# Scores in PSUM banks by row half of the array, and one group's probabilities scaled by ScalarE

## The chip, the cores and the metric

The kernel runs on one core of a Trainium2 chip. The metric is the device time of one execution in microseconds: 998.45 us is the median of three runs of the kernel before (997.99 to 999.91). The engines are named as in the profile: PE is TensorE's matmul side and PEld its weight loads, DVE is VectorE, ACT is ScalarE, POOL is GpSimd and SP is SyncE, which only issues transfers here.

## The reference, cut to what matters

Four layers are added to `x` (64 elements of a batch, 64 tokens each, 512 wide) one after the other. The change lies in the third, attention over a window of 256 earlier keys and the tokens' own 64:

```
q, k, v = x @ Wq.T, x @ Wk.T, x @ Wv.T          # 8 heads of q, 4 groups of k and v, 64 wide
q, k = rope(rms(q)), rope(rms(k))
k_blocks, v_blocks = paged cache with the new k and v written in
scores = einsum('bghtd,bgsd->bghts', q, k_all) * SCALE
scores = where(kpos <= pos and kpos > pos - 256, scores, -inf)
p = softmax(scores)
o = einsum('bghts,bgsd->bghtd', p, v_all)
x = x + o @ Wo.T
x = x + einsum('bct,bcd->bdt', x, weights[subjects]) + bias[subjects]
```

## The kernel before

**Two phases.** Phase one, the first 524 us, works on pairs of elements: expert matmul, adapter, the projections to q, k and v, and the write of the new keys and values to DRAM. Phase two, the rest, takes one element `b` at a time through `phase_two(b, j, s)`, written once for each engine. Every engine runs its own list in the order of the text; only semaphores tie the lists together. An element's stages are spread over several steps: step `b` of TensorE computes the scores of `b`, transposes the probabilities of `b - 1`, and multiplies them with the values of `b - 1`. Below, "even" and "odd" are the parity of `b`, and an element's time is that of its scores.

**TensorE's step.** `scores` (L755), the first half of the next element's keys transposed (`transpose_keys`, L732 and L733), in even steps six matmuls of the output projection (`project`, L803), the ten transposes of the probabilities (L771 for the two blocks of the tokens' own keys into `ps_pt2`, L778 for the eight others into `ps_pt`), the second half of the keys, then in odd steps six matmuls of the projection and in even steps the last layer's matmul (L839), and last `values` (L791, L796), whose last matmul raises `pv_done`.

**The scores.** Each of the four groups `g` has a score of 128 rows (two heads, 64 tokens) by `NK` = 320 keys. Queries and keys of groups 0 and 2 lie in partitions 0 to 63, those of 1 and 3 in 64 to 127, so matmuls of the two kinds use different row halves of the array and run at the same time. A PSUM bank holds 512 columns. `S0` says where a group's 320 columns begin; a group that crosses a bank's edge is computed in two pieces. Before, group 0 lies in bank 0, group 2 in banks 0 and 1, group 3 in banks 1 and 2, group 1 in bank 2: bank 1 gets columns from both halves of the array. So the piece of group 2 in bank 1 raises `s_shared`, and before the last piece, that of group 3 in bank 1, TensorE waits for `s_shared`, which it has raised itself.

**VectorE's step.** `masked(g)` (L1243) adds the mask to a group's scores and finds the extreme; it waits for all four `s_done` of the element and raises `sm_ready`. Between these lie the last layer's sum (L1255, odd steps), `copy_first` (L1225), which takes the first of the transposed probabilities out of PSUM, and the residual sum (L1268, even steps). Then come `recip` (L1276), four products that scale each group's probabilities (L1280, `prob_ready`), `make_mask` for the next element, and last `split_outputs` (L1232, `ot_lo`), which waits for ScalarE's `ot_hi`. The next step's `masked(0)` stands right behind `split_outputs`.

**ScalarE's step.** The first half of the keys copied (L921), the exponentials (L931), `copy_own` and `copy_second` (L943, L938), the second half of the keys, and last `ot_hi` (L968), the rounded output of `b - 1`, which waits for `pv_done`.

**GpSimd** issues the indirect transfers that gather keys and values (L501 from the cache, L537 and L548 from the new rows). They are paced by `pt_done`, `kt_done`, `prob_ready` and `s_done`.

## Time and profile before

| | |
|---|---|
| median of three runs | 998.45 us |
| the profiled execution's own time | 999.21 us |
| its span, first to last instruction | 997.4 us |
| phase two, from the first scores | 524.2 us to the end |
| PE busy | 941.9 us, 94% of the span |
| DVE, ACT, POOL busy | 602.1, 386.0, 512.9 us |
| mean granted TensorE clock | 0.991 of full speed |

The profile is of one execution. A line such as L755 is a line of the kernel file; a group of instructions is named by line, engine, operation and the tiles it writes and reads. Busy time is not the bound by itself: what counts is what an engine waited for before it started, which the views of waits and the timeline tell. Ends of matmuls are modelled in this profile, so a matmul's start is firmer than its end. A wait is put down to the event that the profile saw last; "remote" means that it saw none that fits.

### The profile page before, as it was taken

The page shows a single profiled execution, that of the slowest core. Times are in us where ns is not written, and L with a number is a line of the kernel's source. Part 1 is how long each engine was busy: PE and PEld are TensorE (multiplying, and loading weights), DVE is VectorE, ACT ScalarE, POOL GpSimd, SP SyncE. Part 2 cuts the span into 40 slices and gives each one's busy share as a digit, 9 for nine tenths or more (in the row PEclk, how much of TensorE's full clock was granted, in tenths as well). Part 3 has the DMA queues.
Part 4 walks back from the last instruction along what each step waited for, and adds up shares of the span by engine and source line. Part 5 has one row for each costly group of instructions (what it writes and reads, how often), then busy time and mean ns, then how long its engine had stood idle before and what let it go on. Part 6 is the DMA issues. An engine that isn't in the chain of part 4 may idle for free.

```text
span 997.4 us, 22018 instructions
## 1 busy us (share of the span) xinstructions
PE 941.9 (94%) x6253; PEld 683.0 (68%) x6253; DVE 602.1 (60%) x1788; ACT 386.0 (39%) x1061; POOL 512.9 (51%) x469
## 2 busy tenths in 40 slices
PE   5899999999999999999977999999899999999997
PEld 4566766766766766766755777777677777777775
DVE  5434434656656644356455667776676777677775
ACT  2122122221221221221225556565565656565653
POOL 1245555455455477564565455555455555555530
PEclk9999999999999999999999999999999999999999
DMA  9879877767777667778355565566466565566641
GB/s 299 271 260 315 294 277 265 261 217 271 247 229 274 235 235 260 239 245 281 133 171 172 155 194 165 182 188 184 142 186 190 161 211 192 167 181 191 201 137 44
DMA packets 96458, 212.48 MB, mean 213 GB/s; under 512 B 29051, under 2 KB 35160, under 8 KB 88226
## 3 DMA queue, kind: packets, MB, share of 16 engines
q1 hardware_dynamic: 66434, 145.53, 43.7%
q0 software_dynamic: 25088, 57.74, 19.8%
q10 hardware_dynamic: 4896, 8.73, 2.4%
q8 instruction: 17, 0.28, 0.1%
q14 instruction: 23, 0.19, 0.1%
HBM read 204.39 MB, written 33.86 MB: 239 GB/s over the span
## 4 chain that ended last, share of the span: by engine, by line
PE 91%; DVE 2%; issue 2%; DMA 2%; ACT 1%; another core or an unknown queue 1%; SPq 1%; POOL 0%; ACTq 0%; DVEq 0%; POOLq 0%
PE banks L589 11%; PE banks L755 10%; PE banks L803 10%; PE banks L707 9%; PE banks L791 6%; PE banks L628 6%; PE banks L636 6%; PE banks L638 6%; PE banks L778 5%; PE banks L732 3%; PE banks L839 3%; PE banks L697 3%; PE banks L712 3%; PE banks L796 2%; PE banks L599 2%
## 5 line engine op out<-in xcount | busy, mean ns | idle before, releaser
L548 POOL DMA_INDIRECT ring<-new_rows,idx x128 | 130.8, 1022 | 85.0 <-DVE big L1280 33.9
L460 POOL TENSOR_TENSOR rms<-ss,neg_half 128x12 f32<-128x12 f32 x31 | 70.8, 2284 | 182.0 <-DVE ss L1185 181.0
L931 ACT ACTIVATE big<-big,neg_max 128x320 f32<-128x320 f32 x256 | 141.6, 555 | 5.1 <-DVE neg_max L1243 3.8
L1243 DVE CUSTOM_DVE_ANT_0 big<-banks,mask 128x320 f32<-128x320 f32 x256 | 114.6, 486 | 17.7 <-PE banks L755 13.1
L755 PE MATMUL banks<-kt,q_in 64*128 64x192 f32 (+2 forms) x768 | 103.7, 366 | 20.9 <-remote 12.3
L589 PE MATMUL banks<-ring 128*64 128x512 f32 x512 | 117.1, 599 | 3.0 <-DMA ring<-in_w 3.0
L872 ACT ACTIVATE x2t_hi<-banks 128x512 fp32r<-128x512 f32 x32 | 19.1, 597 | 235.7 <-PE banks L599 235.7
L755 PEld LDWEIGHTS banks<-kt,q_in 64*128 64x128 f32 x768 | 79.0, 188 | 44.5 <-remote 16.9
L501 POOL DMA_INDIRECT ring<-in_kvrows,idx x64 | 61.1, 955 | 63.3 <-PE banks L755 45.8
L537 POOL DMA_INDIRECT ring<-new_rows,idx x64 | 61.4, 960 | 57.7 <-PE banks L778 36.2
L589 PEld LDWEIGHTS banks<-ring 128*64 128x64 f32 x512 | 33.9, 136 | 81.4 <-issue 80.3
L921 ACT ACTIVATE kt<-banks 128x384 f32<-128x384 f32 x128 | 61.8, 483 | 69.6 <-PE banks L733 55.3
L1280 DVE TENSOR_SCALAR big<-big,recip 128x320 f32<-128x320 f32 x256 | 84.2, 392 | 2.3
L791 PEld LDWEIGHTS banks<-pt,ring 128*64 128x64 f32 x1024 | 54.9, 136 | 39.3 <-DVE pt L1225 22.0
L1138 DVE TENSOR_TENSOR x<-banks,x_in 128x512 f32<-128x512 f32 x32 | 22.1, 691 | 95.4 <-PE banks L589 93.8
L791 PE MATMUL banks<-pt,ring 128*64 128x128 f32 x1024 | 70.0, 279 | 4.0 <-ACT pt L938 1.9
L968 ACT ACTIVATE ot_hi<-banks 128x256 fp32r<-128x256 f32 x64 | 24.5, 383 | 120.9 <-remote 67.7
L1232 DVE TENSOR_TENSOR ot_lo<-banks,ot_hi 128x256 fp32r<-128x256 f32 x64 | 27.0, 421 | 73.3 <-ACT ot_hi L968 59.0
L904 ACT ACTIVATE sq<-banks 128x512 f32<-128x512 f32 x31 | 18.5, 597 | 130.6 <-PE banks L638 130.6
L778 PE MATMUL banks<-ident,big 128*128 128x128 f32 x512 | 67.9, 277 | 0.2 <-DVE ot_lo L1232 0.2
L636 PE MATMUL banks<-wqkv_hi,x2t_lo 128*128 128x512 f32 x248 | 66.4, 390 | 0.0
L638 PE MATMUL banks<-wqkv_lo,x2t_hi 128*128 128x512 f32 x248 | 66.3, 389 | 0.0
(169 smaller groups left out, 2015.3 us busy)
## 6 DMA issues: line engine op xcount, KB each, us to landing
ring<-in_w SPq DMA_DIRECT2D x62, 1024.0 KB, 6.4
ring<-in_xt SPq DMA_DIRECT2D x32, 256.0 KB
x_in<-in_x SPq DMA_DIRECT2D x32, 256.0 KB, 5.5
bias_in<-in_b SPq DMA_DIRECT2D x64, 128.0 KB, 5.5
x_dram<-x SPq DMA_DIRECT2D x32, 256.0 KB, 5.1
q_dram<-q_t ACTq DMA_DIRECT2D x32, 256.0 KB
new_rows<-kv_out SPq DMA_DIRECT2D x32, 256.0 KB, 5.0
q_in<-q_dram SPq DMA_DIRECT2D x32, 256.0 KB
```

The lines of the kernel that those rows point to most:

```text
L548: pool.indirect_dma_start(out=kv[:, s, c, :], out_offset=None, in_=new_rows, in_offset=bass.IndirectOffsetOnAxis(ap=idx[:, b, 1 + c:2 + c] ...
L589: last = nc.tensor.matmul(ps_l0[T * h:T * h + T, :], xt[:, s, c, T * h:T * h + T], w0[:, 2 * s + h, c * D:(c + 1) * D], start=(c == 0), st ...
L636: nc.tensor.matmul(ps_out[:, :], x2t_lo[:, c, :], wqkv_hi[:, c, n0:n0 + D], start=False, stop=False)
L638: last = nc.tensor.matmul(ps_out[:, :], x2t_hi[:, c, :], wqkv_lo[:, c, n0:n0 + D], start=False, stop=(c == DC - 1))
L707: nc.tensor.matmul(ps_l1[:, :], x_part[:, c, :], w_part[:, c, :], start=(c == 0 and x_part is x1t_hi and w_part is w1_hi), stop=False)
L755: return nc.tensor.matmul(banks[:, S0[g] + n0:S0[g] + n1], q_in[r0:r0 + HD, s % 4, g // 2, :], kt[r0:r0 + HD, s % 2, g // 2, k0 + n0:k0 + ...
L778: last = nc.tensor.transpose(ps_pt[p][:, (q * 2 + c) * P:(q * 2 + c + 1) * P], prob[:, r % 2, (5 * p + 3 * q + c) * P:(5 * p + 3 * q + c + ...
L791: nc.tensor.matmul(ps_o[p][HD * q:HD * q + HD, :], kv[:, r, c, v0:v0 + HD], pt[:, p, PLACE[2 * p + q] % 2, c, :], start=(c == 0), stop=Fal ...
L803: last = nc.tensor.matmul(out[:, n0:n1], o_part[:, pair_s, c, :], w_part[:, c, n0:n1], start=(c == 0 and n == 0), stop=(c == DC - 1 and n ...
L931: nc.scalar.activation(prob[:, s % 2, PLACE[g] * NK:(PLACE[g] + 1) * NK], sm[:, s % 2, g, :], ACT.Exp, bias=neg_max[:, s % 2, g:g + 1], sc ...
L1243: V.tensor_tensor_reduce(sm[:, s % 2, g, :], ps_s[g], mask[:, s % 2, k0:k0 + NK], 1.0, 3.0e38, ALU.add, ALU.min, accum_out=neg_max[:, s % ...
L1280: V.tensor_scalar(own_row, own_row, recip[:, s % 2, g:g + 1], None, ALU.mult).then_inc(prob_ready, 1)
```

## The change

Four things change together.

- `S0` and the order of the pieces: groups 1 and 3 (the upper row half) now lie in banks 0 and 1, groups 2 and 0 (the lower half) in banks 2 and 3. No bank gets columns from both halves. `s_shared` and TensorE's wait for it are gone. There are six pieces as before, of the same sizes, now in pairs of equal size, one of each half.
- Bank 3 now holds the last 128 columns of group 0, so the transposed keys (`ps_kt`) move from bank 3 to bank 6, and the transposes of the own keys' probabilities (`ps_pt2`) from bank 6 into the rest of bank 3. Those two transposes now stand between the first four and the last four of the others, and wait for `sm_ready` of the same step's `masked(0)`, which reads bank 3.
- The waits of ScalarE's `copy_own` and VectorE's `copy_first` follow the new order of the transposes.
- Group 0's probabilities are scaled by ScalarE, in place, between the second copy of the keys and `ot_hi`; VectorE scales the other three. `prob0_ready` tells TensorE and VectorE of it.

```
-S0 = (0, 3 * BANK - NK, NK, 3 * BANK - 2 * NK)
+S0 = (2 * BANK + NK, 0, 2 * BANK, NK)
...
-        ps_kt, ps_pt, ps_pt2, ps_x = ps[3], ps[4:6], ps[6][:, 0:GP * P], ps[7]
+        ps_kt, ps_pt, ps_pt2, ps_x = ps[6], ps[4:6], ps[3][:, P:P + GP * P], ps[7]
...
-                        pool.wait_ge(prob_ready, G * n + 2)
+                        pool.wait_ge(prob_ready, (G - 1) * n + 2)
...
-                    piece(2, BANK - NK, NK).then_inc(s_shared, 1)
-                    piece(1, 0, NK).then_inc(s_done, 1)
-                    piece(0, 0, NK).then_inc(s_done, 1)
-                    piece(3, P, NK)
-                    piece(2, 0, BANK - NK).then_inc(s_done, 1)
-                    pe.wait_ge(s_shared, b + 1)
-                    piece(3, 0, P).then_inc(s_done, 1)
+                    for g in (2, 1):
+                        piece(g, 0, NK).then_inc(s_done, 1)
+                    for g in (0, 3):
+                        piece(g, 0, BANK - NK)
+                    for g in (0, 3):
+                        piece(g, BANK - NK, NK).then_inc(s_done, 1)
...
-                    pe.wait_ge(prob_ready, G * b)
-                    wait(pe, pt2_ready, b - 1)
-                    for p in range(GP):
-                        last = nc.tensor.transpose(ps_pt2[:, p * P:(p + 1) * P], prob[:, r % 2, (5 * p + 2) * P:(5 * p + 3) * P], ident[:, :])
-                    last.then_inc(pt_done, 1)
+                    pe.wait_ge(prob_ready, (G - 1) * b)
+                    pe.wait_ge(prob0_ready, b)
...
+                        if p == 0:
+                            wait(pe, pt2_ready, b - 1)
+                            if on(b, 0, NB):
+                                pe.wait_ge(sm_ready, G * b + 1)
+                            for n in range(GP):
+                                last = nc.tensor.transpose(ps_pt2[:, n * P:(n + 1) * P], prob[:, r % 2, (5 * n + 2) * P:(5 * n + 3) * P],
+                                                           ident[:, :])
+                            last.then_inc(pt_done, 1)
...
-                    act.wait_ge(pt_done, 3 * b - 2)
+                    act.wait_ge(pt_done, 3 * b - 1)
...
+                if on(b, 0, NB):
+
+                    act.wait_ge(recip_ready, b + 1)
+                    first_row = prob[:, s % 2, PLACE[0] * NK:(PLACE[0] + 1) * NK]
+                    nc.scalar.activation(first_row, first_row, ACT.Copy, scale=recip[:, s % 2, 0:1]).then_inc(prob0_ready, 1)
...
-                    dve.wait_ge(pt_done, 3 * b - 1)
+                    dve.wait_ge(pt_done, 3 * b - 2)
...
-                    wait(dve, prob_ready, G * b - G)
+                    wait(dve, prob_ready, (G - 1) * b - (G - 1))
+                    wait(dve, prob0_ready, b - 1)
...
-                    for g in range(G):
+                    for g in range(1, G):
```

On TensorE, in an odd step of the loop, these rows stand before, from the scores to the second keys (`big` holds the probabilities, `ring` the gathered keys):

```order
L755 MATMUL banks<-kt,q_in 128x128 [waits kt_ready]
L755 MATMUL banks<-kt,q_in 128x320 x2
L755 MATMUL banks<-kt,q_in 128x192 x2
L763 REGISTER_ALU
L755 MATMUL banks<-kt,q_in 128x128 [waits s_shared]
L252 REGISTER_ALU [waits g_new4,g_old4]
L732 MATMUL banks<-ident,ring 128x128 [waits kt_ready]
L732 MATMUL banks<-ident,ring 128x128
L733 MATMUL banks<-ident,ring 128x2x64
L771 MATMUL banks<-ident,big 128x128 [waits pt2_ready,prob_ready]
L771 MATMUL banks<-ident,big 128x128
L778 MATMUL banks<-ident,big 128x128 [waits pt0_ready,ot_ready]
```

And the same place now, where L774 is what L778 was, and L782 what L771 was:

```order
L755 MATMUL banks<-kt,q_in 128x192 x2
L755 MATMUL banks<-kt,q_in 128x128 x2
L252 ISA [waits g_new4,g_old4]
L732 MATMUL banks<-ident,ring 128x128 [waits kt_ready]
L732 MATMUL banks<-ident,ring 128x128
L733 MATMUL banks<-ident,ring 128x2x64
L767 REGISTER_ALU
L774 MATMUL banks<-ident,big 128x128 [waits ot_ready,pt0_ready,prob0_ready,prob_ready]
L774 MATMUL banks<-ident,big 128x128 x3
L780 REGISTER_ALU [waits pt2_ready]
L782 MATMUL banks<-ident,big 128x128 [waits sm_ready]
L782 MATMUL banks<-ident,big 128x128
```

The wait for `s_shared` in front of the last piece is gone. A wait for `sm_ready` has come seven transposes behind the scores (three of keys, four of probabilities); six transposes of probabilities stand behind it.

On ScalarE, at the end of an odd step, these rows stand before:

```order
L921 ACTIVATE kt<-banks 128x384 [waits s_done,kt_done]
L252 REGISTER_ALU [waits pv_done]
L968 ACTIVATE ot_hi<-banks 128x4x64 [waits wo_done]
L919 ISA
L252 ISA [waits kt_done]
```

and these now:

```order
L925 ACTIVATE kt<-banks 128x384 [waits s_done,kt_done]
L970 ACTIVATE big<-big,recip 128x320 [waits recip_ready]
L252 REGISTER_ALU [waits pv_done]
L977 ACTIVATE ot_hi<-banks 128x4x64 [waits wo_done]
L923 ISA
L252 ISA [waits kt_done]
```

The scaling of group 0 (L970) has come in front of `ot_hi`, behind the copy of the keys.

## Rows read from the trace of the kernel before

**Rows 1.** The page: the chain that ended last, by engine.

```profile
PE 91%; DVE 2%; issue 2%; DMA 2%; ACT 1%; another core or an unknown queue 1%; SPq 1%; POOL 0%; ACTq 0%; DVEq 0%; POOLq 0%
```

**Rows 2.** Waits of TensorE: engine, line and who was waited for; us in all, times, longest.

```profile
PE banks L755 <- remote: 12.3, 13, 2.4
...
PE banks L755 <- PE banks L755: 6.1, 14, 0.6
```

**Rows 3.** Timeline: start us, us, engine, line, operation [idle before <-releaser]; one odd element.

```profile
574.71 0.45 PE L796 MATMUL banks<-pt,ring 64*64 64x128 f32 x8
...
575.09 1.35 PE L755 MATMUL banks<-kt,q_in 64*128 64x128 f32 x10
...
575.45 1.01 POOL L548 DMA_INDIRECT ring<-new_rows,idx  x1 [0.30 <-issue]
...
576.42 0.38 ACT L968 ACTIVATE ot_hi<-banks 128x256 fp32r<-128x256 f32 x1 [2.46 <-PE banks L796]
...
576.83 0.42 DVE L1232 TENSOR_TENSOR ot_lo<-banks,ot_hi 128x256 fp32r<-128x256 f32 x1 [1.95 <-issue]
...
577.16 0.49 PE L755 MATMUL banks<-kt,q_in 64*128 64x128 f32 x2 [0.72 <-remote]
...
577.77 0.49 DVE L1243 CUSTOM_DVE_ANT_0 big<-banks,mask 128x320 f32<-128x320 f32 x1 [0.51 <-PE banks L755]
...
579.05 0.38 PE L732 MATMUL banks<-ident,ring 128*128 128x128 f32 x2
```

**Rows 4.** Timeline: the next odd element.

```profile
591.33 0.48 PE L755 MATMUL banks<-kt,q_in 64*128 64x128 f32 x2 [0.56 <-PE banks L755]
...
591.34 0.38 ACT L968 ACTIVATE ot_hi<-banks 128x256 fp32r<-128x256 f32 x1 [3.32 <-remote]
...
591.76 0.42 DVE L1232 TENSOR_TENSOR ot_lo<-banks,ot_hi 128x256 fp32r<-128x256 f32 x1 [2.49 <-ACT ot_hi L968]
...
592.18 0.49 DVE L1243 CUSTOM_DVE_ANT_0 big<-banks,mask 128x320 f32<-128x320 f32 x1
...
593.22 0.38 PE L732 MATMUL banks<-ident,ring 128*128 128x128 f32 x2
```

**Rows 5.** Timeline: the even element between the two.

```profile
582.28 1.35 PE L755 MATMUL banks<-kt,q_in 64*128 64x128 f32 x12
...
582.62 0.38 ACT L968 ACTIVATE ot_hi<-banks 128x256 fp32r<-128x256 f32 x1 [0.59 <-PE banks L796]
...
583.94 0.49 DVE L1243 CUSTOM_DVE_ANT_0 big<-banks,mask 128x320 f32<-128x320 f32 x1
...
585.35 0.38 PE L771 MATMUL banks<-ident,big 128*128 128x128 f32 x2
...
586.44 0.38 PE L732 MATMUL banks<-ident,ring 128*128 128x128 f32 x2
...
586.88 0.96 POOL L537 DMA_INDIRECT ring<-new_rows,idx  x1 [1.23 <-PE banks L778]
```

**Rows 6.** Timeline of one long stop, and its 7 us by engine, clock and DMA.

```profile
713.78 0.48 PE L755 MATMUL banks<-kt,q_in 64*128 64x128 f32 x2 [2.36 <-remote]
...
714.64 0.49 DVE L1243 CUSTOM_DVE_ANT_0 big<-banks,mask 128x320 f32<-128x320 f32 x1
...
718.50 0.59 PE L732 MATMUL banks<-ident,ring 128*128 128x128 f32 x2
...
714.00:721.00 7.00, 7.00 (x42) 5.48 (x41) 5.32 (x18) 4.11 (x13) 2.67 (x3) 0.76 0.36 85
```

**Rows 7.** The page: groups by line, busy us, mean ns of one, idle before.

```profile
L1280 DVE TENSOR_SCALAR big<-big,recip 128x320 f32<-128x320 f32 x256 | 84.2, 392 | 2.3
...
L931 ACT ACTIVATE big<-big,neg_max 128x320 f32<-128x320 f32 x256 | 141.6, 555 | 5.1 <-DVE neg_max L1243 3.8
```

**Rows 8.** Timeline: the last element's probabilities, scaled and transposed.

```profile
982.25 1.27 DVE L1280 TENSOR_SCALAR big<-big,recip 128x320 f32<-128x320 f32 x4
...
983.58 0.44 PE L771 MATMUL banks<-ident,big 128*128 128x128 f32 x2 [1.04 <-DVE big L1280]
```

More of the change, by code:

```diff
@@ L214, in build @@
         g_new = [sem(f"g_new{i}") for i in range(KV_SLOTS)]
-        s_shared, s_done, kt_done, pt_done, pv_done = sem("s_shared"), sem("s_done"), sem("kt_done"), sem("pt_done"), sem("pv_done")
+        s_done, kt_done, pt_done, pv_done = sem("s_done"), sem("kt_done"), sem("pt_done"), sem("pv_done")
         wo_done, l3_done = sem("wo_done"), sem("l3_done")
@@ L220, in build @@
         x3_ready, x4_ready = sem("x3_ready"), sem("x4_ready")
-        e_ready, kt_ready, prob_ready = sem("e_ready"), sem("kt_ready"), sem("prob_ready")
+        e_ready, kt_ready, prob_ready, prob0_ready = sem("e_ready"), sem("kt_ready"), sem("prob_ready"), sem("prob0_ready")
         st_out = [sem(f"st_out{i}") for i in range(2)]
```

## The prediction

> **What bounds the kernel now.** I read the chain that ended last first: 91% of it is TensorE [rows 1], so what counts is TensorE's work and the few places where it stands. The waits of TensorE come next. Its largest waits in the whole kernel are both at L755, the scores: 12.3 us in 13 places put to "remote" and 6.1 us in 14 put to L755 itself, 18.4 us in 27 places [rows 2]. That is the most that the removed wait can be seen to cost. Last I read the timeline of phase two, element by element, and there the parity matters.
>
> In an even element all twelve score instructions (each piece is two) run through in 1.35 us with no stop; `masked(0)` starts 1.66 us behind the scores' start and the probabilities' transposes only 3.07 us behind it, since six projection matmuls lie between [rows 5]. In an odd element ten of the twelve run, TensorE stands for 0.72 us, and the last piece starts at 577.16, 2.07 us behind the start [rows 3]. The signal that it waits for belongs to the first piece, which was through some 1.5 us before. Not only that signal is late. `values` ended at 575.16 (574.71 + 0.45) and `ot_hi`, which needs only its signal and an idle ScalarE, starts at 576.42. In the next odd element `ot_hi` starts at 591.34, after 3.32 us of idle time, and TensorE's last piece at 591.33, at the same moment [rows 4]. So in odd elements TensorE's signals reach everybody late, all at once, and they do so just behind a run of GpSimd's gathers (L548 to 576.46 [rows 3]). That is a time which the change doesn't touch: this run of gathers begins with L537 at 586.88, released by the transposes of the even element before [rows 5].
>
> **The self wait.** It goes with its 0.72 or 0.56 us of standing. What is late next is the new wait: TensorE runs on through three transposes of keys and four of probabilities and then needs `masked(0)` of the same element. In an odd element `masked(0)` hangs on the same late signals twice: through all four `s_done`, and through `pv_done`, `ot_hi` and `ot_lo`, since `ot_lo` stands right in front of it on VectorE. So I compare one point of the step, the start of the second keys (second L732), behind which both kernels do the same.
>
> Second kind of odd element, `pv_done` as late as the rest [rows 4]: `ot_lo` 591.76 + 0.42 = 592.18 = start of `masked(0)`, both before and now. It takes 0.49. From VectorE's end to TensorE's next start there are 0.06 us (L1280 ends at 982.25 + 1.27, L771 starts at 983.58 [rows 8]). Then six transposes at 0.11 each (ten take 586.44 - 585.35 = 1.09 [rows 5]) and 0.06 for the first after a stop (0.44 for two in [rows 8] against 0.38 in [rows 5]): 592.18 + 0.49 + 0.06 + 0.66 + 0.06 = 593.45. Before it was 593.22. The change loses 0.23 here. In about half of these elements `ot_hi` follows its signal faster by up to 0.08, and the loss is 0.16; mean 0.20.
>
> First kind, `pv_done` early enough [rows 3]: `ot_lo` ended at 577.25, and `masked(0)` waited till 577.77 for the last piece, which was behind the self wait. Now it waits for the late signals alone, about 577.35: 577.35 + 0.49 + 0.06 + 0.72 = 578.62 against 579.05. The change gains 0.4 here.
>
> Counted along the timeline from 575 to 970 us, the first kind comes 4 times (scores at 575.09, 631.6, 688.5 and 949.0) and the second 23 times. Sum: 23 x 0.20 - 4 x 0.4 = 4.7 - 1.6 = +3.1 us. The odd elements at 543.8 and 561.4, of the start of phase two, add about 0.2 each: +0.4.
>
> **The long stops.** At two even elements (scores at 550.7 and 710.1) the signals are later still; at the second TensorE stands 2.36 us, and in the 7 us behind it the granted clock is 0.76 on average, below its 2.4 GHz level for part of the time [rows 6]. There the projection lies in front of the new wait, so TensorE works while it would have stood: second keys at 714.64 + 0.49 + 0.06 + 0.72 = 715.91, against 718.50, of which part is the low clock. Worth 1.2 us without the clock and 2.6 with it, each; but which parity a long stop hits is chance. I take half of 2 x 1.2: -1.2. In odd elements such a stop brings the 0.2 as above.
>
> **Even elements.** The new wait is over before it is reached: `masked(0)` ends at 583.94 + 0.49 = 584.43, the transposes that need it come after 585.35 [rows 5]. 0.
>
> **The scaling.** VectorE saves one of four products, 84.2 / 256 = 0.33 us each [rows 7]. VectorE waits in odd elements before `ot_lo` (1.95 and 2.49 us idle [rows 3, 4]), so the saving is lost there; in even ones it starts `masked(0)` a little earlier, which nobody on the path waits for. ScalarE gets 64 products of 128 x 320. No row shows this operation on ScalarE; the nearest are L931, the same tile with an exponential and a sum (0.555 us [rows 7]), and L968, half as many columns from PSUM (0.38 [rows 3]). I take 0.5. It lies in front of `ot_hi`, where ScalarE idles 0.59 us at the tightest place shown [rows 5] and 2.46 or 3.32 in odd ones [rows 3, 4]. Cost 0; at 0.555 with its start it just fits 0.59. If that cover is short by 0.1 us in even elements, `ot_lo` still isn't the last thing that `masked(0)` needs to be early for, as above. At the very end TensorE waits for the scaling [rows 8]: three products end 0.33 earlier while ScalarE does the fourth beside them: -0.2, taken once. The bounds of the whole edit are -0.4 and, if every odd `ot_hi` came 0.1 later, +2.7.
>
> The Trainium skill, page "VectorE: DVE Perf Modes", section "The TRN2 errata — SBUF-src ops pay a fixed extra latency per instruction", speaks against this move: it gives ScalarE 224 cycles plus a cycle per element at 1.2 GHz for SBUF to SBUF, VectorE 58 plus the elements at 0.96 GHz. For 320 elements that is 0.45 us on ScalarE against 0.39 on VectorE, an estimate from that page. By it the product would cost more engine time where it goes than where it leaves, and the sum would be the same, since 0.45 fits the idle time too.
>
> **The pieces.** Same six sizes, both halves get 640 columns as before, and the halves already ran side by side (1.35 us for all [rows 5]). 0; bounds -0.1 and +0.1 an element, -6 and +6 in all, of which I expect nothing since an even element shows no gap. The moved tiles cost nothing by themselves. The first two `s_done` come a little earlier, but L501 waits for late signals in odd elements and for GpSimd itself in even ones: 0.
>
> **The sum.** 3.1 + 0.4 - 1.2 - 0.2 = +2.1 us on 999.21, the profiled execution's own time; its span of 997.4 grows by as much. The median of the runs shown is 998.45, 0.76 lower, so I predict 998.45 + 2.1 = 1000.6 us. For a single measurement of this kernel 0.2%, 2.0 us, is what can be told from no change, and the forecast lies at that edge.
>
> **Rivals.** *The late signals go with the wait* (faster). Then an odd element is like an even one: `masked(0)` 1.66 us behind the scores, seen 0.55 later at 2.21; TensorE is there at 1.35 + 7 x 0.11 = 2.12 and waits 0.1. 18.4 - 27 x 0.1 = 15.7 gained: 983 us. For it: late signals and a standing TensorE come in the same elements. Against it: in even elements, with no stop, `ot_hi` also starts only 0.34 us behind the scores' start (582.62 against 582.28 [rows 5]), though its source is done before them, and in odd ones the lateness ends just behind the gathers. A milder form, in which all odd elements become of the first kind, gives 27 x 0.4 = 11: 988 us.
>
> *The clock* (slower). TensorE's idle time in an odd element moves behind the seven transposes and grows by 0.2 us, to 1.0 to 1.4. A stop of 2.36 us was followed by half-level clock for part of the next 7 us [rows 6], 0.24 x 7 = 1.7 us of full speed lost. If stops of 1.4 us did the same, even in a third of the odd elements, that is 9 x 1.7 = 15: 1016 us. Against it: the mean granted clock is 0.991 over the whole span, with 27 stops of 0.7 us on average in it. [...]
>
> *The array itself is late*, not the signals, so the change doesn't free what it says. The gain of the first kind goes: +1.2 more, 1002 us. Against it: the late signals arrive together while the pieces' starts are spread over 1.3 us. The Trainium skill, page "Perfetto Trace Analysis", section "Tensor Engine Instruction (MATMUL, LD_WEIGHTS)", says that a matmul's end in a profile is an estimate and its signal is pushed when PSUM has acknowledged the writes. By that rule the array may be the late one, and the sum would be this rival's; the trace here doesn't decide it.
>
> **Chances.** Forecast 0.66 (own range 998 to 1003: slower in 0.32, same in 0.30, faster in 0.04). Late signals gone, in either form, 0.20, all faster. Clock 0.07, all slower. Array late 0.07, slower 0.05 and same 0.02. So faster 0.24, same 0.32, slower 0.44. The range runs from 988, the milder form, to 1005.
>
> **What would show it.** Right: in odd elements ten rows become twelve with no gap, TensorE then stands at L782 for about 1.2 us put to VectorE's L1252, and the second keys start 3.7 to 4.3 us behind the scores. `ot_hi` in odd elements still starts 1.3 us or more behind the scores' start. Wrong: no wait at L782 above 0.2 us, or an odd `ot_hi` 0.3 us behind; or a granted clock clearly below 0.99; or gaps before `ot_hi` in which ScalarE is busy with L970.

## The result, and the profile after

The change makes the kernel slower by 0.44%: the ratio of after to before is 1.0044, 95% interval 1.003 to 1.0059, so 4.4 us (3.0 to 5.9). The medians of 20 runs each are 1003.81 us after and 998.56 before; two of after's runs were disturbed, at 3032.14 and 1522.51 us, and count in no comparison (the median of the other 18 is 1003.10). In a later set of runs the same two kernels gave 1.0043 (1.0023 to 1.0062). I had said 1000.6 us, +2.1: the direction and the range hold, the size is half of what was measured. The span of the profiled execution is 1002.8 us, 5.4 more than before, with a mean granted clock of 0.997 (before 0.991); over the 18 runs of after that count it lies between 0.990 and 0.997.

The chain that ended last, by engine, first. Before it was TensorE for 91% [rows 1].

```profile
PE 71%; issue 9%; ACT 8%; another core or an unknown queue 6%; DVE 4%; DMA 2%; SPq 1%; ACTq 1%; DVEq 0%
```

A fifth of the span has gone from TensorE to others and to "issue". Something that TensorE waits for is now on the path. Its waits (line, who was waited for, us in all, times, longest):

```profile
PE banks L774 <- DVE ot_lo L1241: 28.8, 31, 1.4
...
PE banks L843 <- DVE bias_in L1277: 5.3, 16, 0.6
...
PE banks L755 <- issue: 4.0, 4, 1.7
...
PE banks L782 <- DVE neg_max L1252: 0.4, 2, 0.2
```

The 18.4 us at L755 [rows 2] have become 4.0. In their place stand 28.8 us in 31 places at L774, the first four transposes of the probabilities, and they are put to `ot_lo`. The wait that I had named, L782 for `masked(0)`, has 0.4 us, in no place more than 0.2. The prediction names just that as a sign of being wrong ("no wait at L782 above 0.2 us"), and it has come. The timeline of the odd element that answers to [rows 4] (start us, us, engine, line, operation, idle before and releaser):

```profile
589.50 1.01 POOL L548 DMA_INDIRECT ring<-new_rows,idx  x1 [0.30 <-issue]
...
589.64 1.35 PE L755 MATMUL banks<-kt,q_in 64*128 64x320 f32 x12
...
590.93 0.44 PE L732 MATMUL banks<-ident,ring 128*128 128x128 f32 x2
...
591.38 0.38 ACT L977 ACTIVATE ot_hi<-banks 128x256 fp32r<-128x256 f32 x1 [2.46 <-remote]
...
591.80 0.42 DVE L1241 TENSOR_TENSOR ot_lo<-banks,ot_hi 128x256 fp32r<-128x256 f32 x1 [2.51 <-ACT ot_hi L977]
...
592.22 0.49 DVE L1252 CUSTOM_DVE_ANT_0 big<-banks,mask 128x320 f32<-128x320 f32 x1
...
592.48 0.63 PE L774 MATMUL banks<-ident,big 128*128 128x128 f32 x4 [1.00 <-DVE ot_lo L1241]
...
592.94 0.38 PE L782 MATMUL banks<-ident,big 128*128 128x128 f32 x2
...
593.16 0.60 PE L774 MATMUL banks<-ident,big 128*128 128x128 f32 x4
...
593.60 0.38 PE L732 MATMUL banks<-ident,ring 128*128 128x128 f32 x2
```

The twelve score rows run through with no gap. The signals are as late as they were: `ot_hi` (L977) starts 1.74 us behind the scores. TensorE is through with the first keys at about 591.3 and then stands for `ot_ready`, which `ot_lo` raises (591.80 + 0.42), until 592.48. L782 follows 0.46 us behind the first of the four transposes, with hardly a wait. From `ot_hi` to the second keys it takes 593.60 - 591.38 = 2.22 us; before it was 593.22 - 591.34 = 1.88 [rows 4]. I call an element late when its `ot_hi` starts more than 1.1 us behind its scores; behind 570 us these are 27 after and 28 before, all odd but the one of the long stop. Their median is 2.21 after and 1.95 before: +0.26 us.

The median hides that before had the prediction's two kinds. In the 22 elements of the second kind of [rows 4] that are late in both kernels the way was 1.91 us on average (1.87 or 1.96 each) and is 2.22 now, +0.31 each. In the four of the first kind of [rows 3] it was 2.64 and is 2.21, -0.43 each. After has only one kind left. Summed over the elements it is +6.9 and -1.7, together +5.2 us.

The even element, for [rows 5]:

```profile
581.80 0.55 ACT L970 ACTIVATE big<-big,recip 128x320 f32<-128x320 f32 x1
...
582.32 1.36 PE L755 MATMUL banks<-kt,q_in 64*128 64x320 f32 x12
...
582.58 0.38 ACT L977 ACTIVATE ot_hi<-banks 128x256 fp32r<-128x256 f32 x1 [0.23 <-PE banks L800]
...
585.40 0.60 PE L774 MATMUL banks<-ident,big 128*128 128x128 f32 x4
...
586.49 0.38 PE L732 MATMUL banks<-ident,ring 128*128 128x128 f32 x2
```

Up to the second keys it is as before within 0.05 us (586.49, before 586.44). ScalarE's scaling (L970) ends 0.23 us ahead of `ot_hi`, which starts 0.26 us behind the scores (before 0.34).

Element by element, the scores of the two kernels start together at 575.1 us. At the element of the long stop they are 2.7 us apart (710.1 and 712.8), behind it 0.3 (728.0 and 728.4), and at the last element 5.3 (976.66 and 981.97). That is 0.28 us in each pair of elements, 9.5 pairs and 17.5 pairs, with 2.4 us won at the one long stop between: 7.6 us lost elsewhere.

Where those 7.6 us lie depends on where one measures from. From scores to scores, the 28 odd elements grew by 1.1 us in all and the 27 even ones (without that of the long stop) by 6.1, of which some 5.4 lie between an even element's second keys and the next scores. There the residual sum (L1277) starts 4.09 us behind the scores in the median, before 3.82, and TensorE waits for it. But beside that stretch run the gathers that lead to the next late signal: L537 begins behind the even element's transposes, and the odd `ot_hi` comes 4.25 us behind it on average. So I cut the same time at the signals, in 26 pairs of elements without the one of the long stop:

| after minus before, us in 26 pairs | first trace of after | second trace of after |
|---|---|---|
| odd second keys to even transposes | -0.9 | -0.9 |
| to the start of L537 | -0.9 | -1.2 |
| to the odd `ot_hi` | +3.6 | +0.1 |
| `ot_hi` to the odd second keys | +5.7 | +5.9 |
| together | +7.5 | +3.9 |

Only the way from `ot_hi` to the second keys grows by the same amount in both traces. The time from L537 to `ot_hi` differs by as much between the two executions of after as between one of them and before. That the even elements' wait for the residual sum costs nothing of its own, because it runs beside the gathers, is my reading of this table. It isn't shown: no run takes that wait away alone, and where the time from L537 to the odd scores is longer, that from L537 to `ot_hi` tends to be longer too.

The groups that answer to [rows 7], the long stop of [rows 6] and the end of [rows 8]:

```profile
L1290 DVE TENSOR_SCALAR big<-big,recip 128x320 f32<-128x320 f32 x192 | 63.1, 385 | 2.4
...
L970 ACT ACTIVATE big<-big,recip 128x320 f32<-128x320 f32 x64 | 36.0, 562 | 2.2 <-DVE recip L1286 0.7 <-issue 0.5
```

```profile
712.76 1.36 PE L755 MATMUL banks<-kt,q_in 64*128 64x320 f32 x12
...
716.19 0.39 ACT L977 ACTIVATE ot_hi<-banks 128x256 fp32r<-128x256 f32 x1 [3.24 <-remote]
...
717.28 0.63 PE L774 MATMUL banks<-ident,big 128*128 128x128 f32 x4 [0.37 <-DVE ot_lo L1241]
...
718.40 0.38 PE L732 MATMUL banks<-ident,ring 128*128 128x128 f32 x2
```

```profile
989.16 0.63 PE L774 MATMUL banks<-ident,big 128*128 128x128 f32 x4 [1.32 <-DVE ot_lo L1241]
```

### The profile page after: what moved, and what is told of

The parts are those of the page before. It is cut to its first block, busy times and chain, and to the rows that moved or that the text cites. A ratio compares the mean times of both kernels' runs of the same rounds, so it can differ in the third digit from the quotient of the medians.

```text
span 1002.8 us, 22139 instructions
## 1 busy us (share of the span) xinstructions
PE 930.4 (93%) x6253; PEld 665.0 (66%) x6253; DVE 583.9 (58%) x1724; ACT 419.5 (42%) x1125; POOL 515.0 (51%) x469
## 4 chain that ended last, share of the span: by engine, by line
PE 71%; issue 9%; ACT 8%; another core or an unknown queue 6%; DVE 4%; DMA 2%; SPq 1%; ACTq 1%; DVEq 0%
PE banks L589 11%; PE banks L707 8%; PE banks L807 6%; PE banks L628 6%; PE banks L636 6%; PE banks L638 6%; PE banks L795 4%; PE banks L774 4%; PE banks L800 3%; ACT big L935 3%; PE banks L697 3%; PE banks L712 3%; PE banks L755 3%; PE banks L599 2%
## 5 line engine op out<-in xcount | busy, mean ns | idle before, releaser
L548 POOL DMA_INDIRECT ring<-new_rows,idx x128 | 131.3, 1026 | 83.0 <-PE banks L755 37.9
L774 PE MATMUL banks<-ident,big 128*128 128x128 f32 x512 | 77.8, 274 | 28.8 <-DVE ot_lo L1241 28.8
L537 POOL DMA_INDIRECT ring<-new_rows,idx x64 | 61.6, 962 | 65.4 <-PE banks L774 56.9
L755 PE MATMUL banks<-kt,q_in 64*128 64x320 f32 (+2 forms) x768 | 88.7, 362 | 4.0 <-issue 4.0
L774 PEld LDWEIGHTS banks<-ident,big 128*128 128x128 f32 x512 | 59.5, 141 | 39.6 <-issue 33.2
L755 PEld LDWEIGHTS banks<-kt,q_in 64*128 64x128 f32 x768 | 66.4, 188 | 25.1 <-issue 15.8
L450 POOL TENSOR_TENSOR x_in<-x_in,bias_in 128x512 f32<-128x512 f32 x32 | 41.0, 1280 | 54.8 <-DMA ring<-in_rope 48.1
```

The source lines that it names most:

```text
L548: pool.indirect_dma_start(out=kv[:, s, c, :], out_offset=None, in_=new_rows, in_offset=bass.IndirectOffsetOnAxis(ap=idx[:, b, 1 + c:2 + c] ...
L755: return nc.tensor.matmul(banks[:, S0[g] + n0:S0[g] + n1], q_in[r0:r0 + HD, s % 4, g // 2, :], kt[r0:r0 + HD, s % 2, g // 2, k0 + n0:k0 + ...
L774: last = nc.tensor.transpose(ps_pt[p][:, (q * 2 + c) * P:(q * 2 + c + 1) * P], prob[:, r % 2, (5 * p + 3 * q + c) * P:(5 * p + 3 * q + c + ...
```

## The experiments

All carry a short edit of one of the two kernels. Beside each ratio I give what the trace says of one point, the way from the start of `ot_hi` to the second keys in the late elements (median of 27 to 29): 1.95 us before, 2.21 after. The ratios' intervals are some 0.5% wide, so most of them don't tell one edit from another; this way does.

**The scaling taken back.** The kernel after, with VectorE scaling all four groups.

```
-                    first_row = prob[:, s % 2, PLACE[0] * NK:(PLACE[0] + 1) * NK]
-                    nc.scalar.activation(first_row, first_row, ACT.Copy, scale=recip[:, s % 2, 0:1]).then_inc(prob0_ready, 1)
...
-                    pe.wait_ge(prob_ready, (G - 1) * b)
-                    pe.wait_ge(prob0_ready, b)
+                    pe.wait_ge(prob_ready, G * b)
...
-                    for g in range(1, G):
+                    for g in range(G):
```

> The kernel after, with VectorE scaling all four groups' probabilities as before; banks, order of the transposes and the missing wait stay as after. Theory A (the loss is where the own-key transposes stand relative to TensorE's wait for ot_ready: they were done in front of it and now lie behind it, 0.22 us and a restart in each of the 27 or so odd elements with late signals): about as after, 3.5 to 5.5 us slower than before, L774 still stands about 1 us on L1241 in odd elements. Theory B (ScalarE's scaling, 0.55 us in front of ot_hi, makes ot_hi late): at most 1 us slower than before. A little may be lost on either by a VectorE step 0.3 us longer.

Ratio to before 1.0032 (1.0009 to 1.0054): most of the loss stays without the scaling, as theory A says, though 3.2 us is a little under its 3.5 to 5.5, and the interval holds after's 1.0044 too. A late element, `ot_lo` and the first transposes:

```profile
604.58 0.42 DVE L1235 TENSOR_TENSOR ot_lo<-banks,ot_hi 128x256 fp32r<-128x256 f32 x1 [2.23 <-ACT ot_hi L971]
...
605.10 0.63 PE L773 MATMUL banks<-ident,big 128*128 128x128 f32 x4 [0.71 <-issue]
```

They start 0.52 us behind the start of `ot_lo` (median 0.53), not 0.68: with one wait less in front of them, 0.15 less. The second keys come 2.11 us behind `ot_hi`. So the scaling has a price after all, but through the wait that it needs and not through its 0.56 us.

**The scaling alone.** The kernel before, with the lines above put in.

> The kernel before, with only the scaling of group 0 given to ScalarE. Theory A (order of the transposes): within 1 us of before. Theory B (ScalarE's scaling): 4 to 5 us slower. In the profile the odd ot_hi (L968) starts as before, 1.3 us or more behind the scores' start, under A; later by up to 0.55 us under B.

Ratio 1.0006 (0.9981 to 1.0031), 1.95 us from `ot_hi` to the second keys: no change. `ot_hi` itself starts 1.97 us behind the scores (before 1.79), but the signal that TensorE's last piece waits for is as late, and from the end of the last gather to `ot_hi` it is 0.74 us (before 0.77), so this is the gathers' timing and not the scaling. The extra wait for `prob0_ready` costs nothing here either, since TensorE is busy when it comes to it. Theory B falls.

**The order alone.** The kernel before, with the transposes in the order of after.

```
                     pe.wait_ge(prob_ready, G * b)
-                    wait(pe, pt2_ready, b - 1)
-                    for p in range(GP):
-                        last = nc.tensor.transpose(ps_pt2[:, p * P:(p + 1) * P], prob[:, r % 2, (5 * p + 2) * P:(5 * p + 3) * P], ident[:, :])
-                    last.then_inc(pt_done, 1)
                     wait(pe, ot_ready, b - 1)
                     for p, copied in ((0, pt0_ready), (1, pt1_ready)):
...
                         last.then_inc(pt_done, 1)
+                        if p == 0:
+                            wait(pe, pt2_ready, b - 1)
+                            for n in range(GP):
+                                last = nc.tensor.transpose(ps_pt2[:, n * P:(n + 1) * P], prob[:, r % 2, (5 * n + 2) * P:(5 * n + 3) * P],
+                                                           ident[:, :])
+                            last.then_inc(pt_done, 1)
```

> The kernel before, with only the order of the transposes changed: the first four of the others, then the two own-key ones, then the last four. Banks and TensorE's wait for itself stay. Theory A: slower by 3 to 6 us, the first transposes stand on ot_lo about 1 us in odd elements and the second keys move 0.2 us back. Theory C (banks, and the new wait for sm_ready, cost the time): no change, within 1 us.

Ratio 1.0023 (0.9998 to 1.0049): slower at the edge of what the runs tell, less than theory A's 3 to 6 us, and 2.06 us from `ot_hi` to the second keys. One late element:

```profile
604.21 0.38 ACT L970 ACTIVATE ot_hi<-banks 128x256 fp32r<-128x256 f32 x1 [3.11 <-remote]
...
604.27 0.48 PE L755 MATMUL banks<-kt,q_in 64*128 64x128 f32 x2 [0.34 <-PE banks L755]
...
604.63 0.42 DVE L1234 TENSOR_TENSOR ot_lo<-banks,ot_hi 128x256 fp32r<-128x256 f32 x1 [2.25 <-ACT ot_hi L970]
...
604.69 0.44 PE L732 MATMUL banks<-ident,ring 128*128 128x128 f32 x2
...
605.15 0.63 PE L774 MATMUL banks<-ident,big 128*128 128x128 f32 x4
```

This shows how the two orders differ. Before, everything behind the late signal is TensorE's own work: last piece, first keys, ten transposes, 1.87 to 1.96 us without a stop. Here the transposes that overwrite `ps_o` come 0.2 us earlier in the list than `ot_ready` allows, and wait about 0.1 us, not the expected 1 us, since the last piece and the keys still stand in front. The expected second keys 0.2 us later were 0.11.

**Fewer waits.** The kernel after without the waits for `pt0_ready`, `pt1_ready` and `pt2_ready` of the element before, which `values` has passed already.

```
-                    for p, copied in ((0, pt0_ready), (1, pt1_ready)):
-                        wait(pe, copied, b - 1)
+                    for p in range(GP):
...
-                            wait(pe, pt2_ready, b - 1)
```

> The kernel after, with the waits for pt0_ready, pt1_ready and pt2_ready of the step before left out in front of the transposes (values of the step before has waited for the same counts), so that ot_ready is the last wait of its row. Theory A with a restart made longer by waits in a chain: the gap from the start of ot_lo to the first transposes falls from 0.68 us by about 0.1, in 27 odd elements, 2 to 3 us faster than after. Rival (the chain of waits costs nothing, only the signal's way counts): as after, within 0.7 us.

Ratio to before 1.0022 (0.9994 to 1.0049), where after has 1.0044 and 1.0043 in its two sets of runs. The interval alone decides nothing; the trace has 0.57 us from `ot_lo` to the transposes and 2.11 from `ot_hi` to the second keys, 0.10 less than after, as expected.

**One wait.** The kernel after with `ot_ready` as the only wait in that row.

```
-                    pe.wait_ge(prob_ready, (G - 1) * b)
-                    pe.wait_ge(prob0_ready, b)
+                    if isinstance(b, int) and b < 2:
+                        pe.wait_ge(prob_ready, (G - 1) * b)
+                        pe.wait_ge(prob0_ready, b)
                     wait(pe, ot_ready, b - 1)
```

> The kernel after, with ot_ready as the only wait in front of the first transposes of the probabilities (four before: prob_ready, prob0_ready, ot_ready, pt0_ready; VectorE raises ot_ready of the element before behind everything that the others stand for), and no waits for pt1_ready and pt2_ready behind them. Theory W (each wait in that row costs TensorE about 0.1 us although it is long fulfilled; the traces so far have 0.45 us with two waits, 0.53 to 0.57 with three, 0.68 with four from the start of ot_lo to the transposes behind it): 0.35 us with one, the second keys 1.9 us behind ot_hi in place of 2.21, 27 times 0.3 = 8 us faster than after, so some 3 us faster than the kernel before. Rival (the number of waits is a coincidence, it is where the own-key transposes stand): 0.6 us or more, not more than 2 us faster than after.

Ratio to before 1.0013 (0.9986 to 1.0039), beside 1.0043 for after on the same chip: some 3 us are won back, not 8, with intervals that overlap.

```profile
602.49 0.42 DVE L1240 TENSOR_TENSOR ot_lo<-banks,ot_hi 128x256 fp32r<-128x256 f32 x1 [2.35 <-ACT ot_hi L976]
...
602.92 0.49 DVE L1251 CUSTOM_DVE_ANT_0 big<-banks,mask 128x320 f32<-128x320 f32 x1
...
602.97 0.66 PE L774 MATMUL banks<-ident,big 128*128 128x128 f32 x4 [0.50 <-DVE ot_lo L1240]
...
603.47 0.44 PE L781 MATMUL banks<-ident,big 128*128 128x128 f32 x2
...
604.19 0.38 PE L732 MATMUL banks<-ident,ring 128*128 128x128 f32 x2
```

The first transposes start 0.48 us behind `ot_lo`, not 0.35. Then L781 comes 0.50 us behind them, where it was 0.46 in after: now it is TensorE's wait for `masked(0)` that holds (602.92 + 0.49, and 0.06 to TensorE's start, is 603.47). With the restart behind it this costs 0.1 us, from the first transposes to the second keys 1.21 us in place of 1.12. So the second keys stay 2.11 us behind `ot_hi`. The wait that I had predicted is there; it lies 0.1 us behind the one that bound.

**One wait, in the kernel before.**

```
                     pe.wait_ge(prob_ready, G * b)
-                    wait(pe, pt2_ready, b - 1)
...
-                    for p, copied in ((0, pt0_ready), (1, pt1_ready)):
-                        wait(pe, copied, b - 1)
+                    for p in range(GP):
```

> The kernel before, with prob_ready as the only wait in front of the own-key transposes and ot_ready as the only one in front of the others (pt0_ready, pt1_ready and pt2_ready left out). Theory W: from ot_lo to the transposes 0.35 us in place of 0.45, second keys 1.85 us behind ot_hi in place of 1.95, 27 times 0.1 = 3 us faster than before. Rival: no difference, within 1 us.

Ratio 0.999 (0.9969 to 1.001), and 0.45 and 1.95 us as before: theory W misses here. In the kernel before TensorE is busy from the late signal on, so there was no wait to shorten. What W said of the number of waits holds only where TensorE stands: 0.48 us with one, 0.53 and 0.57 with three, 0.68 with four.

**After once more**, unchanged.

> The kernel after, unchanged, so that g1 can be compared with it on one chip: 3 to 6 us slower than before on either theory, 0.68 us from ot_lo to the first transposes.

1.0043 (1.0023 to 1.0062), 0.68 us and 2.21 us as in its first trace.

**No bursts of gathers.** The kernel before, without L548, and `g_new` counted accordingly.

```
-                    pool.indirect_dma_start(out=kv[:, s, c, :], out_offset=None, in_=new_rows,
-                                            in_offset=bass.IndirectOffsetOnAxis(ap=idx[:, b, 1 + c:2 + c], axis=0),
-                                            bounds_check=NB * T - 1, oob_is_err=False).then_inc(g_new[s], 16)
...
-                    pe.wait_ge(g_new[s], 48 * (j + 1))
+                    pe.wait_ge(g_new[s], 16 * (j + 1))
```

> The kernel before without the two gathers of new rows in columns 0 and 1 of each element (L548): it leaves the batch's new keys and values out of the windows of earlier keys. All waits of GpSimd stay. Theory G (the bursts of gathers hold TensorE's signals back): no odd ot_hi later than 0.5 us behind the scores' start, odd period about 6 us, whole run 20 to 35 us shorter. Rival S (TensorE's wait for itself holds them): odd ot_hi still 1.3 us behind the scores, no shorter than 3 us.

948.76 us, 47 less than before, more than I expected. An odd element:

```profile
592.98 1.36 PE L752 MATMUL banks<-kt,q_in 64*128 64x128 f32 x12
...
593.12 0.38 ACT L965 ACTIVATE ot_hi<-banks 128x256 fp32r<-128x256 f32 x1 [1.26 <-PE banks L793]
...
594.65 0.38 PE L768 MATMUL banks<-ident,big 128*128 128x128 f32 x2
...
595.74 0.38 PE L729 MATMUL banks<-ident,ring 128*128 128x128 f32 x2
```

`ot_hi` starts 0.14 us behind the scores, the last piece has no gap, and TensorE doesn't stand. An odd period is 5.99 us in the median (7.02 before), an even one 6.87 (7.13). Behind 570 us all of TensorE's late signals but one, in an even element, have gone with the gathers, and the kernel still waits for itself. So the lateness comes with the gathers; rival S falls. Part of the 47 us can be the traffic saved, which this run doesn't separate.

**After without them.** The same edit to the kernel after.

> The kernel after without the two gathers of new rows in columns 0 and 1 of each element (L548): it leaves the batch's new keys and values out of the windows of earlier keys, as the kernel before without them did (948.8 us). If the change costs only where TensorE's signals are late: no odd element stands on ot_lo, 1 us slower to 3 us faster than that. If it costs by itself: 951 us or more.

953.28 us, 4.5 more than the kernel before without them. The change costs by itself too, which I had not expected. An odd element:

```profile
591.48 1.36 PE L752 MATMUL banks<-kt,q_in 64*128 64x320 f32 x12
...
592.03 0.42 DVE L1238 TENSOR_TENSOR ot_lo<-banks,ot_hi 128x256 fp32r<-128x256 f32 x1 [1.10 <-ACT ot_hi L974]
...
593.14 0.49 DVE L1249 CUSTOM_DVE_ANT_0 big<-banks,mask 128x320 f32<-128x320 f32 x1 [0.69 <-PE banks L752]
...
593.14 0.60 PE L771 MATMUL banks<-ident,big 128*128 128x128 f32 x4
...
593.70 0.44 PE L779 MATMUL banks<-ident,big 128*128 128x128 f32 x2
...
594.41 0.27 PE L729 MATMUL banks<-ident,ring 128*128 128x128 f32 x1
```

Here `ot_lo` is long done. `masked(0)` starts as TensorE's first transposes do, at 593.14, and L779 needs its result: 593.70, 0.56 us behind, where four transposes take 0.44. With 0.05 for the restart the second keys come 2.93 us behind the scores, not 2.76. That is 0.17 us in nearly every odd element. From the scores at 573.25 us to those at 915.21 without the change, and from 571.59 to 917.50 with it, the difference is 4.0 us: 26 odd elements by 0.17, less 0.6 won in the one even element where the kernel before had a late signal. The two times, of two runs each and on two chips, are 4.5 apart; as ratios to the kernel before on their own chips they are 0.9524 (0.9478 to 0.9571) and 0.9567 (0.9527 to 0.9607), so the times alone don't show the cost, and the traces do. This is the predicted wait, at the predicted place, in a kernel whose signals are on time.

**A later third gather.** The kernel before, with L548's second gather moved behind the next element's scores.

```
-                        pool.wait_ge(prob_ready, G * n + 2)
+                        pool.wait_ge(s_done, G * (n + 1) + 2)
```

> The kernel before, with the third gather of an element's new rows (L548, c = 1) issued by GpSimd only when the second score piece of the next element is done, so that three gathers no longer run back to back into an odd element's scores. Theory G (TensorE's signals come 0.6 to 1.0 us behind the end of back-to-back gathers): odd ot_hi starts 0.2 to 0.4 us behind the scores as in even elements, the odd period falls from 7.0 us by 0.7 to 1.2, the whole by 15 to 30 us. Rival S (the signals are late because TensorE waits for itself): odd ot_hi as late as before, within 2 us of before. Third case: the gathers behind it now delay another signal, gain below 10 us.

Ratio 1.001 (0.9988 to 1.0032). The odd period falls to 6.13 us as theory G has it, though `ot_hi` still starts 0.98 us behind the odd scores and not 0.2 to 0.4, and the even one rises from 7.13 to 8.23: the third case. The burst has only moved to the even elements. One of them, with its scores at 593.39:

```profile
591.66 0.96 POOL L537 DMA_INDIRECT ring<-new_rows,idx  x1 [0.30 <-issue]
...
593.44 1.00 POOL L548 DMA_INDIRECT ring<-new_rows,idx  x1 [0.82 <-remote]
...
594.23 0.52 PE L755 MATMUL banks<-kt,q_in 64*128 64x320 f32 x1 [0.30 <-issue]
...
594.95 1.11 PE L755 MATMUL banks<-kt,q_in 64*128 64x320 f32 x8 [0.21 <-issue]
...
595.35 0.38 ACT L968 ACTIVATE ot_hi<-banks 128x256 fp32r<-128x256 f32 x1 [2.06 <-remote]
```

Here not only signals are late. The scores themselves have gaps, 0.30 and 0.21 us, at matmuls in front of which no wait stands (the only one is in front of the last piece), and the profile puts them to "issue". In the whole run these are the largest entry of TensorE's waits:

```profile
PE banks L755 <- issue: 18.1, 43, 1.7
```

40 of these gaps, 14.9 us, lie in the even elements behind 575 us. So beside a gather TensorE can be held up itself, which is what the prediction's third rival says (*the array itself is late*). In the trace of before, three such gaps, 0.31 to 0.35 us each, lie in the scores of the first long stop (550.7); behind 575 us neither before nor after has one.

**The same in the kernel after.**

> The kernel after, with the same later third gather. If the signals come on time, the first transposes no longer stand on ot_lo, the loss of the change goes, and its missing wait (about 0.2 to 0.4 us in an odd element) may show: 0 to 8 us faster than the kernel before with the same later gather. If the signals are as late as before: as after, 4 us slower than before.

Ratio to before 1.0006 (0.9983 to 1.0028), beside 1.001 for the kernel before with this edit. So the change costs nothing in all that these runs can tell once the late signals fall into even elements: there six projection matmuls lie between the signals and the transposes. It doesn't pay either. By parity the two traces differ: the odd period is 6.26 us (6.13 without the change), the same 0.1 to 0.2 us lost as without the gathers, and the even one 8.01 (8.23), with late signals in 15 even elements and 6.8 us of gaps in the scores in place of 18.1. Why there are fewer isn't shown.

**The last piece later.** The kernel before, with group 3's last piece and TensorE's wait for itself behind the first transposes of the keys.

```
                 if on(b, -1, NB):
                     transpose_keys(b + 1, j + (s == KV_SLOTS - 1), (s + 1) % KV_SLOTS, 0)
+                if on(b, 0, NB):
+                    last_piece()
```

> The kernel before, with the last score piece (group 3, 128 columns) and TensorE's wait for itself moved behind the first transposes of the keys, which do not need them: the wait has three transposes' time to come in. Theory A (in odd elements the path is late signal, ot_hi, ot_lo, first transposes, and what lies in front hides behind it): at most 2 us faster, none slower than 1. Rival (TensorE's wait for itself is what costs, 18 us of waiting in 64 elements): 6 us or more faster.

Ratio 1.0183 (1.0142 to 1.0224), 18 us slower, against both. The even element shows why:

```profile
583.07 1.35 PE L755 MATMUL banks<-kt,q_in 64*128 64x128 f32 x10
...
584.35 0.44 PE L732 MATMUL banks<-ident,ring 128*128 128x128 f32 x2
...
584.83 0.49 PE L755 MATMUL banks<-kt,q_in 64*128 64x128 f32 x2
...
585.24 0.50 PE L805 MATMUL banks<-wo_hi,ot_hi 128*128 128x512 f32 x1
```

Behind the keys the piece takes 585.24 - 584.83 = 0.41 us, while the scores without it are not shorter: 584.35 - 583.07 = 1.28 us, the same as with it. In its old place it ran beside group 2's piece in the other half of the array, for nothing. The even period rises to 7.68 us from 7.13. For the odd elements the run says what theory A does: with the signals late as ever, from `ot_hi` to the second keys it takes 1.83 us in place of 1.95, a gain of 0.12 and not of the 0.6 for which TensorE had stood.

No version that keeps all the gathers beats the kernel before by more than the runs can tell; the least is 0.999.

## Why the prediction was right, and where it was not

Right was half of the mechanism: the self wait covers late signals and does not make them, and when it goes, TensorE stands at the next instruction that hangs on them. The late signals stayed (`ot_hi` 1.67 us behind the scores in the median), and the rivals "late signals go with the wait" and "the clock" did not come (clock 0.997 in the profile, 0.990 or more in the other runs). Wrong was which instruction that is, and that the sum came out near the measured time is in good part luck, as the ledger below shows. The rival "the array itself is late" is not decided. Its price stands wrongly in the prediction: if the gain of the first kind goes, that is 4 x 0.4 = 1.6 us and 1002.2, not 1.2 and 1002. The gaps in the scores of the run with the later third gather speak for it, the 0.43 us won in the elements of the first kind against it.

The step that failed is "TensorE runs on through three transposes of keys and four of probabilities and then needs `masked(0)`". It can't run through the four of probabilities: they write the banks of `ps_o`, and wait for `ot_ready`. I had followed `ot_lo` only as what stands in front of `masked(0)` on VectorE. In the kernel before that wait was always fulfilled when TensorE came to it, since the last piece, the keys and the two own-key transposes (0.42 + 0.38 + 0.22 us) lay between it and the late signal, so it never appeared in the waits. The change took all three away from there: two run earlier now, one later. The way from the late signal is then 0.42 (`ot_hi`) + 0.42 (`ot_lo`) + 0.26 (signal and four waits) + 1.12 (ten transposes) = 2.22 us, against TensorE's own 1.87 to 1.96.

The terms for the late elements, measured in the prediction's own way from the late `ot_hi`: the second kind loses 0.31 us and not 0.20. Behind the end of `ot_lo` the prediction had 0.49 + 0.06 + 0.72 = 1.27 us, and it took 0.26 + 1.12 = 1.38. The first kind gains 0.43, as forecast (0.4), but not for the reason given: it became an element like all others. Measured from the scores, the gain is smaller. In the four elements the second keys lay 3.96, 4.14, 3.89 and 4.07 us behind the scores and now lie 3.97, 3.88, 4.07 and 3.60 behind, 0.5 us won in all, because their `ot_hi` now starts 1.67 us behind the scores on average and before 1.37. Together it is +5.2 us where the forecast had +3.1.

Of the 0.26 us between the medians, the runs tell the parts: 0.11 is in the order (the kernel before with the new order), and 0.15 lies between `ot_lo` and the transposes, where after has four waits and the new order alone has three (0.68 against 0.53 us). Taking the wait for `prob0_ready` out wins only 0.10 (2.11), for then TensorE comes to `masked(0)` 0.05 us early: from the first transposes to the second keys it takes 1.17 us in place of 1.12.

The ledger, from the two profiled executions (+5.4 us of span), against the sum of the prediction:

| term | forecast | measured |
|---|---|---|
| phase one, up to the first scores | 0 | +0.95 |
| start of phase two, without its long stop | +0.4 | +2.0 |
| the elements behind 575 us, without the long stop | +3.1 | +7.6 |
| the two long stops | -1.2 | -5.3 |
| the end | -0.2 | +0.15 |
| together | +2.1 | +5.4 |

Of the 7.6 us, 5.2 are the way from the late signals; the rest did not come again in the second trace. Two terms are off by 4 us and more in opposite directions. The prediction itself called the long stops chance, and took half of them; a version with the right wait and this price for the long stops would have forecast hardly any loss.

The long stops: at the first (scores at 550.7) the period fell from 10.75 to 7.79 us, but after's first scores were 1.0 us later to begin with and the elements at 536 and from 561 on lost another 2.3, so that both kernels pass 575.1 together. The one at 710 gave 1.9, and 0.5 in the element behind it. I had -1.2 for both, and they gave 5.3. The element at 536 is even and had a late signal too (`ot_hi` 2.46 us behind its scores); I had left it out. In the long stop of after TensorE's row starts at 717.28, 1.09 us behind `ot_hi`, and the second keys at 718.40.

Even elements: no wait at the new place, as said. But TensorE's wait for the residual sum (`bias_in`, L843) grew to 5.3 us in 16 places; before it was 2.6 us in 5 places, at L839. The prediction put nothing there. It lies between the even transposes and the late signal of the odd element, so by the table above it need not cost, but that isn't shown by a run of its own.

The scaling: 0.56 us on ScalarE (36.0 us / 64), above my 0.5 and at my upper row of 0.555. In the even element shown it left 0.23 us idle. VectorE's saving, 84.2 - 63.1 = 21.1 us, moved nothing. The Trainium skill, page "VectorE: DVE Perf Modes", section "The TRN2 errata — SBUF-src ops pay a fixed extra latency per instruction", gave 0.45 us as an estimate; the trace has 0.56. For VectorE the prediction worked out 0.39 from the same section of the Trainium skill, and the trace has 0.392 and 0.385. The formula there divides the elements by a perf-mode factor, which the prediction took as 1 without saying so. What I missed is that handing a product to another engine adds a semaphore to a row in which TensorE stands.

The end: -0.2 did not come. From the last scores to the first transposes it was 983.58 - 976.66 = 6.92 us before and 989.16 - 981.97 = 7.19 after; there too `ot_lo` is what came last.

## What to carry to other kernels

When a wait goes, list every wait between it and the next point that both versions share, also those that show no time now: a wait that was always fulfilled becomes the bound as soon as the work in front of it moves. Work that stands behind a late signal but needs nothing from it hides the way through the other engines; take it from there only if it is on the path. A product moved to an idle engine costs its user one more semaphore, here 0.10 to 0.15 us where the user stands at that place. And cut a loop's time at the event that paces it: cut at the scores, this loss seemed to lie in the even elements.

## What the runs showed of the hardware

TensorE's signals came late where GpSimd had issued gathers back to back. In the runs with all gathers, `ot_hi` in late elements starts 0.67 to 0.81 us (medians of eleven traces; 1.23 in after with the later third gather, where 15 are late) behind the end of GpSimd's last gather; without L548 only one element behind 570 us was late, in the kernel before, and none in after. Moving a gather moved the late signals with it, and with it came gaps inside the scores (18.1 us in 43 places). Whether the signals alone are late or TensorE's work too, and what in the chip joins them to the gathers, isn't shown.

Semaphore waits that are long fulfilled are not free for a standing TensorE: from the start of `ot_lo` (0.42 us) to the transposes behind it 0.48 us with one wait, 0.53 and 0.57 with three, 0.68 with four. In the kernel before, where TensorE has work, taking waits out changed nothing (1.95 us from `ot_hi` to the second keys both times).

A matmul piece of 64 rows by 128 columns cost nothing beside a piece in the other row half (1.28 us for the scores with and without it) and 0.41 us behind transposes, alone.
